# Two-layer graph network on one core: scatter without its 11 empty columns, last count closed within its group, reciprocals in halves, three evacuations moved

## What is computed

```python
def _rgcn(x, edge_index, edge_type, weight, root, bias):
    src, dst = (edge_index[0], edge_index[1])
    msgs = x[src]
    out = x @ root + bias
    for r in range(weight.shape[0]):                   # 8 relations
        mask = (edge_type == r).astype(x.dtype)
        sums = segment_sum(msgs * mask[:, None], dst, n)
        cnt = segment_sum(mask, dst, n)
        mean = sums / jnp.maximum(cnt, 1.0)[:, None]
        out = out + mean @ weight[r]
    return out
u = _rgcn(...)
z = concatenate([u, x], axis=1) @ w_gate + b_gate
h = tanh(u) * z + x * (1.0 - z)
```

## Time and profile before

| | |
|---|---|
| median of 3 runs | 1909.2 us (1906.59 to 1910.06) |
| the profiled execution's own time | 1905.15 us |
| its span (first to last instruction) | 1903.6 us |
| PE busy | 1810.2 us, 95% of the span, 10058 matmuls |
| PE weight loads | 1491.0 us, 78% |
| DVE busy | 1037.8 us, 55% |
| POOL busy | 703.3 us, 37% |
| ACT busy | 484.4 us, 25% |
| DMA | 162.26 MB, mean 85 GB/s |
| the chain that ended last | PE 84%, DVE 6%, ACT 6%, issue 1%, DMA 1% |

### The profile page before, as it was taken

How to read it: one execution, slowest core, us unless ns; L and a number is a source line. 1 busy time by engine, 2 the same in 40 slices (tenths; PEclk the granted TensorE clock), 3 DMA queues, 4 the chain that set the end, 5 groups by cost and what they waited for, 6 DMA issues and landing times.

```text
span 1903.6 us, 28941 instructions
## 1 busy us (share of the span) xinstructions
PE 1810.2 (95%) x10058; PEld 1491.0 (78%) x10058; DVE 1037.8 (55%) x2591; ACT 484.4 (25%) x1073; POOL 703.3 (37%) x609
## 2 busy tenths in 40 slices
PE   6999999999999999999999999954999999999999
PEld 4876689987877778787777877743899888878987
DVE  7888999996354544525354356776632225262311
ACT  3139966662010110101011045333200000111100
POOL 2100000003535435453543543200395553345862
PEclk9999999999999999999999999956999999999999
DMA  4432222223312122231313523110254351123322
GB/s 134 151 102 80 75 83 72 73 72 122 91 41 88 41 74 56 65 92 39 93 39 118 175 78 116 45 45 6 65 172 145 115 152 60 34 56 110 94 73 66
DMA packets 129285, 162.26 MB, mean 85 GB/s; under 512 B 14288, under 2 KB 75368, under 8 KB 128922
## 3 DMA queue, kind: packets, MB, share of 16 engines
q1 hardware_dynamic: 100848, 120.93, 21.2%
q10 hardware_dynamic: 22250, 23.53, 3.9%
q0 software_dynamic: 6080, 16.40, 2.9%
HBM read 135.51 MB, written 25.30 MB: 84 GB/s over the span
## 4 chain that ended last, share of the span: by engine, by line
PE 84%; DVE 6%; ACT 6%; issue 1%; DVEq 1%; DMA 1%; POOL 0%; SPq 0%; ACTq 0%
PE ps L367 21%; PE ps L368 21%; PE ps L369 21%; PE ps L1229 9%; PE ps L890 3%; ACT sc_col L836 2%; ACT sc_row L835 1%; PE ps L1194 1%; DVE w_lo L318 1%; PE ps L879 1%; PE ps L1149 1%; DMA nat<-in_x 1%; ACT w_hi L313 1%; PE ps L1702 1%; PE ps L1176 0%
## 5 line engine op out<-in xcount | busy, mean ns | idle before, releaser
L367 PE MATMUL ps<-w_hi,xt_hi 128*125 128x512 f32 x1320 | 540.0, 409 | 12.6 <-DVE xt_lo L549 3.5
L256 POOL TENSOR_TENSOR w_hi<-w_stage,zero 128x512 fp32r<-128x512 f32 x256 | 277.8, 1085 | 697.4 <-PE ps L369 678.8
L368 PE MATMUL ps<-w_lo,xt_hi 128*125 128x512 f32 x1320 | 523.7, 397 | 0.0
L369 PE MATMUL ps<-w_hi,xt_lo 128*125 128x512 f32 x1320 | 522.3, 396 | 0.0
L259 POOL TENSOR_TENSOR w_lo<-w_stage,w_hi 128x512 fp32r<-128x512 f32 x256 | 346.6, 1354 | 20.0
L367 PEld LDWEIGHTS ps<-w_hi,xt_hi 128*125 128x125 f32 x1320 | 247.2, 187 | 70.7 <-DVE xt_lo L1162 4.6
L369 PEld LDWEIGHTS ps<-w_hi,xt_lo 128*125 128x125 f32 x1320 | 246.5, 187 | 63.4
L368 PEld LDWEIGHTS ps<-w_lo,xt_hi 128*125 128x125 f32 x1320 | 246.9, 187 | 53.4
L367 PE MATMUL ps<-xt_hi,w_hi 128*128 128x314 f32 x736 | 250.5, 340 | 0.8 <-DVE ring L2404 0.7
L369 PE MATMUL ps<-xt_hi,w_lo 128*128 128x314 f32 x736 | 225.9, 307 | 0.0
L368 PE MATMUL ps<-xt_lo,w_hi 128*128 128x314 f32 x736 | 225.7, 307 | 0.0
(11 more groups left out here) (391 smaller groups left out, 2442.2 us busy)
## 6 DMA issues: line engine op xcount, KB each, us to landing
w_stage<-in_stream SPq DMA_DIRECT2D x374, 256.0 KB, 2.7
...
```

Of the source, the lines that this page charges most:

```text
L256: POOL.tensor_tensor(w_hi[:, q, :], w_stage[:, q % NST, :], zero[:].to_broadcast([128, 512]), ALU.add).then_inc(S("hi_done"), 1)
L367: PE.matmul(dst, l_hi, r_hi, start=first, stop=False)
L368: PE.matmul(dst, l_hi, r_lo, start=False, stop=False)
L369: return PE.matmul(dst, l_lo, r_hi, start=False, stop=last)
```

## The change

- The four memsets of the padding are gone, and the scatter of the 11 padded columns on DVE, ACT and PE. These are the columns of the last chunk of group 5. The closing matmul with zeros stands now behind the last real column, at the end of the seventh chunk.
- On DVE the copy of `slot_ps` and the tables of histogram steps 0 and 1 stand in front of the evacuation of group 5.
- The first fold of `scan` is done in two halves of 10 rows, with the evacuation of group 2 between them.
- The rest of histogram step 119 is laid into group 9, two hooks behind its first part.
- The reciprocals are taken for columns 0 to 312 where they all were, and for 313 to 624 behind the first `mtmp` of the relation. The semaphore `rcnt` counts twice in a relation.
- At the end of stage 2, the low part of feed piece 4 stands behind the evacuation of the last group.

```diff
--- before.py
+++ after.py
@@ -700,8 +700,6 @@
 
         DVE.wait_ge(S("ld_edges"), 48)
 
-        for n in (e_col1, e_row1, e_lo, e_hi):
-            DVE.memset(n[:, EC:ECP], -1.0)
         for j in range(4):
             DVE.memset(g_weight[:, :, j], 2.0 ** (6 * j))
 
@@ -786,10 +784,14 @@
         n = NBUCKET
         while n % 2 == 0:
             n //= 2
-            DVE.tensor_tensor(scan[:, 0:n], scan[:, 0:n], scan[:, n:2 * n], ALU.add)
             if 2 * n == NBUCKET:
+                h = n // 2
+                DVE.tensor_tensor(scan[:, 0:h], scan[:, 0:h], scan[:, n:n + h], ALU.add)
                 evacuate(2)
+                DVE.tensor_tensor(scan[:, h:n], scan[:, h:n], scan[:, n + h:2 * n], ALU.add)
                 split_low_dve(31, 32)
+            else:
+                DVE.tensor_tensor(scan[:, 0:n], scan[:, 0:n], scan[:, n:2 * n], ALU.add)
             DVE.drain()
         DVE.tensor_reduce(e_pos[:], scan[:, 0:n].rearrange("p b c -> p c b"), AX.X, ALU.add)
         DVE.drain()
@@ -919,6 +921,7 @@
         natural16()
 
         PE.sem_inc(S("sc_pe"), sc_per)
+        PE.sem_inc(S("hi_pe"), 6)
         zero16 = hot_col[4][0:P, 0:128]
         DVE.memset(zero16, 0.0)
         DVE.memset(hot_col[5][0:P, 0:2 * NCHUNK], 0.0)
@@ -934,8 +937,11 @@
         def scatter_step(i):
             def between(k, m):
                 for j in range(sc_per):
-                    if j * T // sc_per == m:
-                        scatter_pe((i * KT + k) * sc_per + j, j)
+                    c = (i * KT + k) * sc_per + j
+                    if j * T // sc_per == m and c < EC:
+                        scatter_pe(c, j)
+                    if j * T // sc_per == m and c == EC - 1:
+                        PE.matmul(slot_ps, zero16, hot_col[5][0:P, 0:2 * NCHUNK], start=False, stop=True).then_inc(S("sc_pe"), 1)
             return between
 
         SC0, LEAD = 4, 6
@@ -952,27 +958,29 @@
             load_bias(i + SC0)
             for k in range(KT):
                 for j in range(sc_per):
-                    scatter_act((i * KT + k) * sc_per + j, j)
+                    if (i * KT + k) * sc_per + j < EC:
+                        scatter_act((i * KT + k) * sc_per + j, j)
                     if j == 2:
                         split_act(C_HAND + LEAD + i * KT + k)
+        DVE.sem_inc(S("hi_add"), 4)
         for i in range(SC_GROUPS):
             for k in range(KT):
                 for j in range(sc_per):
-                    scatter_dve((i * KT + k) * sc_per + j, j)
+                    if (i * KT + k) * sc_per + j < EC:
+                        scatter_dve((i * KT + k) * sc_per + j, j)
                     if j == 4:
                         split_dve(C_HAND + LEAD + i * KT + k)
+            if i == SC_GROUPS - 1:
+                wait(DVE, mk_zero)
+                DVE.wait_ge(S("sc_pe"), sc_per + EC + 1)
+                DVE.tensor_copy(slot[:, :, 0:NCHUNK], slot_ps.rearrange("p (a c) -> p a c", a=2))
+                DVE.drain()
+                for n in range(2):
+                    hist_dve_hot(n, n)
             evacuate(i + SC0)
 
-        PE.matmul(slot_ps, zero16, hot_col[5][0:P, 0:2 * NCHUNK], start=False, stop=True).then_inc(S("sc_pe"), 1)
-        wait(DVE, mk_zero)
-        DVE.wait_ge(S("sc_pe"), sc_per + ECP + 1)
-        DVE.tensor_copy(slot[:, :, 0:NCHUNK], slot_ps.rearrange("p (a c) -> p a c", a=2))
-        DVE.drain()
-
-        DVE.sem_inc(S("hi_add"), 4)
         ALE.sem_inc(S("hi_rest"), 2)
         ALE.sem_inc(S("hi_main"), 2)
-        PE.sem_inc(S("hi_pe"), 6)
         HI0 = SC0 + SC_GROUPS
         assert HI0 + HI_GROUPS == G_PRE0
         per = NGROUP // HI_GROUPS
@@ -997,6 +1005,8 @@
                 n = hist_of(h, k * T + m)
                 if n is not None:
                     hist_pe(h * per + n, (h * per + n) % 4)
+                if h == HI_GROUPS - 1 and k * T + m == slot_of(h, per - 1) + 2:
+                    hist_pe_rest(NGROUP - 1, (NGROUP - 1) % 4)
             return between
 
         def chunk_at(h, n):
@@ -1006,7 +1016,6 @@
 
         for h in range(HI_GROUPS):
             dense(h + HI0, hist_step(h))
-        hist_pe_rest(NGROUP - 1, (NGROUP - 1) % 4)
         ALE.wait_ge(S("ld_bt"), 16)
         for h in range(HI_GROUPS):
             for n in range(per):
@@ -1022,8 +1031,6 @@
         for i in range(2):
             evacuate_half(HI0 + HI_GROUPS - 1, 3, i)
 
-        for n in range(2):
-            hist_dve_hot(n, n)
         for h in range(HI_GROUPS):
             for n in range(per):
                 g = h * per + n
@@ -1316,7 +1323,11 @@
             DVE.wait_ge(S("ag_full"), r * 18 + i + 2)
             DVE.tensor_scalar(rcnt[:, h0:h0 + hn], ps[:, bank, 0:hn], 1.0, None, ALU.max).then_inc(S("ag_free"), 1)
         DVE.wait_ge(S("ag_free"), 3 + r * 18 + 2)
-        DVE.reciprocal(rcnt[:, 0:NODES], rcnt[:, 0:NODES]).then_inc(S("rcnt"), 1)
+        DVE.reciprocal(rcnt[:, 0:H0], rcnt[:, 0:H0]).then_inc(S("rcnt"), 1)
+
+    def counts_rest(r):
+
+        DVE.reciprocal(rcnt[:, H0:NODES], rcnt[:, H0:NODES]).then_inc(S("rcnt"), 1)
 
     def att_dve_front(r):
 
@@ -1359,7 +1370,7 @@
 
     def relation_dve(r, more):
 
-        DVE.wait_ge(S("rcnt"), r + 1)
+        DVE.wait_ge(S("rcnt"), 2 * r + 1)
 
         def low(j):
             h0, hn = halves[j % 2]
@@ -1377,6 +1388,9 @@
 
             DVE.wait_ge(S("ag_free"), 3 + r * 18 + i + 1)
             DVE.sem_inc(S("ag_scaled"), 1)
+            if j == 0:
+                counts_rest(r)
+                DVE.wait_ge(S("rcnt"), 2 * r + 2)
             if j >= 1:
                 low(j - 1)
         low(15)
@@ -1396,7 +1410,7 @@
                     att_dve_back(r, qkf[:, 0])
                 else:
                     att_dve_back(r, ao[:, :, 7 * 128:8 * 128])
-                    for k in range(5):
+                    for k in range(4):
                         feed_dve(k, k)
             DVE.wait_ge(S(f"ld_u{gg}"), 16)
             for m in range(T):
@@ -1404,6 +1418,8 @@
                 u_ = nat[:, m, gg * 512:(gg + 1) * 512]
                 DVE.wait_ge(S("bank_free"), (r * 2 + g0) * T + T)
                 DVE.tensor_tensor(u_, u_, ps[0:P, m, :], ALU.add).then_inc(S("bank_free"), 1)
+        if not more:
+            feed_dve(4, 4)
 
     def degrees():
 
```

## The result

The changed kernel took 1891.35 us in the median of 4 runs (1890.8 to 1892.73), the kernel before 1909.58 beside it (1906.59 to 1910.06): a ratio of 0.9913, 95% interval 0.9901 to 0.9926. 18.2 us were won; the sum said 11.3, the predicted 1897.9 is 6.5 too high, and the range began at 1893.5. The two profiled executions differ by less, 12.4 us (1905.15 and 1892.73). So two questions stand: which terms of the sum were off inside the pair of traces, and where the other 5.8 us are, which the pair doesn't show.

A forecast was written before the change was run, and what follows sets the result against it. PE, busy 95% of the span, was taken as the bound. Terms 3.3 + 3.85 + 1.5 + 0.2 + 2.4, rounded to 11.3, off 1905.15 gave 1893.9; plus 4.05, 1897.9 us; range 1893.5 to 1903.

The forecast's parts named there:

- the last one of the sum: Whole kernel: from the profiled execution's forecast of 1893.9 us to the median of runs, adding 4.05, giving 1897.9 us.
- the stretch at 113: Start of group 3: half clock on PE behind the wait for bank 0 would go, 1.6 us.
- The clock rival: Remaining waits at groups 4, 5, 6 and stage 2 draw half clock, 1.6 us each; two give 1901.1 us; chance 0.15.
- The last count: End of stage 1, PE's 2.61 us wait: a_hi starts after group 9's last matmul, 1.5 us won; earlier signal, up to 2.6.
- The scatter: Last chunk of group 5 to the histogram: no padded columns and earlier tables, 3.85 us won; bounds 2.4 and 4.7.
- the fold: End of group 2: evacuation after half a fold saves 1.7 us of wait and 1.6 of half clock, together 3.3.
- new wait: Before group 6: PE idles 0.9 us because the evacuation of group 5 stands behind the tables on DVE.
- The rival that the tables ahead of the evacuation cost what they save: Group 6: PE loses at the bank what the histogram gains, 2.0 instead of 3.85 us; total 1900.3; chance 0.13.
- The reciprocals: Entry to stage 2: halves make the first mtmp 2.03 us earlier, but the second is late; 0.2 us won.
- the rival on the slow side: Stage 2: the second half of the reciprocals costs up to 4.07 us, eight mtmps come later, 1913.3 us; chance 0.03.
- The feed: End of stage 2: evacuation ahead of piece 4's low part removes PE's wait for bank 0, 2.4 us won.
- given back later: Projection's second group: weights from ACT, POOL and DMA don't move up, 2.4 us lost, 1900.3 us; chance 0.09.

The follow-up runs named there:

- the first profile: The profiled execution of the unchanged kernel before, taken beside the change: 1905.15 us, with half clock behind the waits at 113, 145 and 197.
- v_tab: The changed kernel with the count's tables of step 1 behind the evacuation again, no fillers: 1890.5 us beside 1891.15 for the changed kernel.
- e_recip: The kernel before with only the reciprocals in halves: median 1905.94 us beside 1908.81 for the kernel before.
- e_feed: The kernel before with only the evacuation of ao put in front of its feed: median 1905.76 us beside 1909.51 for the kernel before.

## Why the prediction was wrong, step by step

**The step that failed is the last one of the sum**: "The median of the runs, 1909.2, lies 4.05 above that execution; I take the same difference from it: 1897.9 us." The 4.05 us were no fixed offset that both kernels carry. For the most part they were half clock behind waits that the change removes: 1.5 us at 249, 1.7 at 447, 1.4 to 2.1 at 1115. Where each trace has the old wait, six of eight drew it at 249, two of ten at 447 and six of ten at 1113, and the first profile drew none of the three. Weighted so they make 2.7 us, and 0.6 more is the first profile's early start; for unprofiled executions this is inferred. The sum priced only the stretch at 113, since of the three in the trace (113, 145 and 197) it was the only one behind a wait that the change removes.

What it should have done is price the removed waits by what they draw in the usual execution, which one trace couldn't show, and leave the offset out: that gives 1893.9, which is 1.2 above the changed kernel's profiled execution and 2.5 above its median. The 18.2 us of the medians are the pair's 12.4, plus 4.4 by which the median of before lies above its profile, plus 1.4 by which that of the changed kernel lies below its own. This 1.4 is of the size of the draws around 1320 us (1.3), which the changed kernel's profile had and two of its three later ones hadn't. The sum had added 4.05 us to the changed kernel's side, where 1.4 had to be taken off.

**The clock rival had the right mechanism and the wrong sign.** It saw that half clock isn't tied to the length of a wait and that the three runs spanned 3.5 us "as such draws would make them", and then charged it to the changed kernel. The rule of the Trainium skill that it named (TensorE: Matmul & The Clock Gate, What's actually happening), that the count of slow matmuls varies between runs of one kernel, is borne out by the four traces of one kernel: 3, 3, 5 and 6 short stretches before 1200 us. It says nothing of the price, which goes by place.

**The last count** was mis-sized, 1.5 for 2.7. Of its two cases the sum took the one in which PE's signal comes with the last matmul, for want of a row; the other, up to 2.6, is what happened.

**The scatter** (3.85, measured 3.7) and **the fold** (3.3, measured 3.4, the half clock with it) were right, with their parts: chunk 4.43 for 4.5, new wait 0.59 for 0.9, idle at the fold 0.36 for 0.4. The rival that the tables ahead of the evacuation cost what they save is refuted in size, and v_tab shows what may be true of it, 0.5 to 0.8 us.

**The reciprocals** (0.2, measured 0.1 in the pair and -0.2 in e_recip): the second halves fit beside the aggregations, and the reciprocal is priced by its elements, 2.10 to 2.12 us for half of 4.07, also beside POOL, which splits weights from 433.8 on. So the rival on the slow side is out. The subtraction beside POOL took 1.40 us (0.49 without it, at 439.52), and with the second mtmp late PE kept 1.25 + 0.43 of its 2.11.

**The feed** (2.4, measured 2.7, in e_feed 1.2): right, with some of "given back later": nine of the twenty traces have 0.2 to 1.2 us of wait for a weight chunk there, where that rival had 2.4 in all. The premise that all behind a wait is released by PE's own progress is off by that much.
